# Six attention phases in a slot pipeline: one score round with 64 rows and 512 columns, v by one full-array product, layer normalisation on ScalarE

## The reference

```
def _mha(q, k, v, mask, ...):
    Q, K, V = (t @ w + b).reshape(b, s, H, DK).transpose(0, 2, 1, 3)   # for each of the three
    scores = einsum('bhqd,bhkd->bhqk', Q, K) / sqrt(DK)
    scores = where(mask[:, None] == 0, -1e20, scores)
    A = softmax(scores, axis=-1)
    return einsum('bhqk,bhkd->bhqd', A, V).transpose(0, 2, 1, 3).reshape(b, sq, D) @ wo + bo

def _ln(x, g, b):
    m, v = mean(x, -1), var(x, -1)
    return (x - m) * rsqrt(v + 1e-5) * g + b
```

## Time and profile before

| | |
|---|---|
| median of 3 runs | 714.12 us (712.08 to 714.96) |
| the profiled execution | 715.84 us, of which its span is 714.0 us |
| PE busy | 660.5 us (92% of the span) |
| DVE / ACT / POOL busy | 510.5 / 455.2 / 320.0 us |
| chain that ended last | PE 71%, issue 14%, POOL 7% |

### The profile page before, as it was taken

The page is one execution under the profiler, slowest core; times in us unless marked ns, Lnnn a source line. Parts: engine busy times, 40 slices in busy tenths (PEclk is TensorE's granted clock), DMA queues, the critical chain, the costliest instruction groups (busy, mean ns, idle before and its releaser), DMA issues.

```text
span 714.0 us, 26835 instructions
## 1 busy us (share of the span) xinstructions
PE 660.5 (92%) x9470; PEld 468.4 (66%) x9470; DVE 510.5 (71%) x1259; ACT 455.2 (64%) x1274; POOL 320.0 (45%) x540
## 2 busy tenths in 40 slices
PE   1999999999999999999999849899997899999995
PEld 1566666677777766666666536799993556666773
DVE  0599899878788778888888743344433788988884
ACT  1366777677777787777777533455524667777874
POOL 2244444467666653333377564255433345442110
PEclk9999999999999999999999769999995899999998
DMA  8333343322332310101011000122232000000100
GB/s 268 104 93 88 85 94 79 73 64 50 78 96 84 104 54 25 29 24 32 24 43 37 25 31 31 50 67 64 68 90 81 24 25 23 22 17 17 36 28 27
DMA packets 48527, 42.07 MB, mean 59 GB/s; under 512 B 6553, under 2 KB 42909, under 8 KB 47280
## 3 DMA queue, kind: packets, MB, share of 16 engines
q1 hardware_dynamic: 41632, 23.33, 11.6%
q10 hardware_dynamic: 4528, 13.25, 7.5%
q0 software_dynamic: 2272, 4.24, 1.9%
HBM read 25.41 MB, written 14.79 MB: 56 GB/s over the span
## 4 chain that ended last, share of the span: by engine, by line
PE 71%; issue 14%; POOL 7%; DVE 3%; ACT 2%; ACTq 1%; DMA 0%; SPq 0%; POOLq 0%; DVEq 0%
PE ps L570 11%; PE ps L607 10%; PE ps L738 5%; PE ps L811 5%; PE ps L800 5%; PE ps L663 5%; PE ps L644 4%; PE ps L680 4%; PE ps L746 4%; PE ps L719 3%; POOL k_by_j L500 3%; PE ps L664 2%; PE ps L766 2%; PE ps L592 2%; PE ps L691 2%
## 5 line engine op out<-in xcount | busy, mean ns | idle before, releaser
L1106 DVE TENSOR_REDUCE top<-ps 128x16 f32<-128x1024 f32 (+1 forms) x96 | 108.9, 1134 | 41.9 <-PE ps L570 40.2
L492 POOL TENSOR_TENSOR rstd<-spread,half_neg 128x1 f32<-128x1 f32 x80 | 44.5, 557 | 194.4 <-DVE spread L1199 115.2
L500 POOL TENSOR_TENSOR k_by_j<-k_t,cst 128x512 f32<-128x512 f32 (+1 forms) x96 | 95.5, 995 | 74.2 <-ACT k_t L915 37.8
L570 PE MATMUL ps<-k_by_j,q_t 32*64 32x256 f32 (+1 forms) x1536 | 125.2, 396 | 1.1
L607 PE MATMUL ps<-cst,prob 128*128 128x128 f32 x704 | 120.3, 291 | 1.1 <-ACT prob L936 1.0
L607 PEld LDWEIGHTS ps<-cst,prob 128*128 128x128 f32 x704 | 77.2, 144 | 62.0 <-issue 45.6
L1065 DVE RECIPROCAL inv<-ps 128x128 f32<-128x128 f32 x96 | 91.8, 956 | 32.3 <-PE ps L746 30.0
L1122 DVE TENSOR_TENSOR prob<-ps,top 128x1024 f32<-128x1024 f32 (+1 forms) x96 | 108.3, 1128 | 0.7
L936 ACT ACTIVATE prob<-prob 128x1024 f32<-128x1024 f32 (+1 forms) x96 | 94.8, 987 | 22.0 <-DVE prob L1122 21.7
L885 ACT ACTIVATE prob_t<-ps 128x512 f32<-128x512 f32 (+1 forms) x96 | 53.9, 561 | 38.7 <-PE ps L607 38.3
L873 ACT ACTIVATE prob_t<-ps 128x512 f32<-128x512 f32 (+1 forms) x96 | 53.9, 561 | 29.6 <-PE ps L607 28.5
(11 more groups left out here) (155 smaller groups left out, 1202.4 us busy)
## 6 DMA issues: line engine op xcount, KB each, us to landing
sorted_rows<-zero_rows ACTq DMA_DIRECT2D x32, 276.2 KB, 2.7
stage_m<-in_m SPq DMA_DIRECT2D x80, 64.0 KB, 1.9
mow<-in_mow SPq DMA_DIRECT2D x18, 256.0 KB, 3.0
stage_kv<-in_ctx_t SPq DMA_DIRECT2D x64, 64.0 KB, 1.7
rows_in<-sorted_rows SPq DMA_DIRECT2D x39, 65.0 KB, 1.8
wat<-in_wat ACTq DMA_DIRECT2D x1, 1280.0 KB, 6.5
x_t<-in_x_t SPq DMA_DIRECT2D x16, 64.0 KB, 1.9
stage_kv<-in_x_t SPq DMA_DIRECT2D x16, 64.0 KB, 1.7
```

What stands on the lines that cost most here:

```text
L500: pool.tensor_tensor(k_by_j[:, p, 0:nj, :], k_t[:, p:p + 1, :].broadcast_to([128, nj, TOK]), cst[:, cj:cj + nj].unsqueeze(2).broadcast_to( ...
L570: mm = pe.matmul(ps[S * b:S * b + S, 2 * p + bank, r * nj * S:(r + 1) * nj * S].rearrange("p (h k) -> p h k", k=S), q_t[rows_g, p, S * b:S ...
L1106: dve.tensor_reduce(top[:, p, 0:nh].rearrange("p (b h) -> p b h", b=2), sc, AX.X, ALU.max).then_inc(top_d, 1)
```

## The change

Three edits. **Scores:** `k_by_j` gets 8 copies for 16 heads (4 for 8 heads) in place of 4 (2). The scores are one round of four products with 64 rows and 512 columns (256 in phase 5) in place of two rounds of four with 32 rows and 256 (128) columns, and it stands whole at the head of the slot. Its waits are moved into the slot before, between the two groups of the last product (`score_ready(following)`). **v:** one product of the full array with 128 columns in place of four with 64 output columns; the copies to `v_16` and `v_8` then go from partition half b to half par, four in each phase (before: four with 16 heads, two with 8). **Normalisation:** in phases 0, 1 and 4 `normed` moves from DVE to ACT, as rstd*y + shift, where shift = -mean*rstd is made by two more small operations on POOL.

```
@@ gpsimd @@
                     pool.tensor_tensor(rstd[:, p, :], spread[:, p, :], half_neg[:, :], ALU.pow)\
                         .then_inc(rstd_d, 1)
+                    if POST[pr.phase] == "ln":
+                        pool.tensor_tensor(minus[:, p, :], none[:, :], moments[:, p, 0:1], ALU.subtract).then_inc(minus_d, 1)
+                    ...
+                        wait_pair(pool, minus_d, pr)
+                        wait_pair(pool, rstd_d, pr)
+                        pool.tensor_tensor(shift_n[:, p, :], minus[:, p, :], rstd[:, p, :], ALU.mult).then_inc(shift_d, 1)
                 pr = at(OFF_PROJ)
                 if pr is not None:
-                    p, nj = pr.p, heads(pr) // 4
+                    p, nj = pr.p, heads(pr) // 2
...
                     pool.tensor_tensor(k_by_j[:, p, 0:nj, :], k_t[:, p:p + 1, :].broadcast_to([128, nj, TOK]),
@@ tensor @@
+            def score(pr):
+                p, nj = pr.p, heads(pr) // 2
                 masked = MASKED[pr.phase]
                 for bank in range(2):
-                    rows_g = slice(32 * (2 * bank + r), 32 * (2 * bank + r) + 32)
+                    rows_h = slice(S * bank, S * bank + S)
                     for b in range(2):
                         mm = pe.matmul(
-                            ps[S * b:S * b + S, 2 * p + bank, r * nj * S:(r + 1) * nj * S].rearrange("p (h k) -> p h k", k=S),
-                            q_t[rows_g, p, S * b:S * b + S], k_by_j[rows_g, p, 0:nj, S * b:S * b + S],
-                            start=not masked and r == 0, stop=True, skip_group_check=True)
+                            ps[S * b:S * b + S, 2 * p + bank, 0:nj * S].rearrange("p (h k) -> p h k", k=S),
+                            q_t[rows_h, p, S * b:S * b + S], k_by_j[rows_h, p, 0:nj, S * b:S * b + S],
+                            start=not masked, stop=True, skip_group_check=True)
+                mm.then_inc(score_d, 1)
...
-                        scored = at(OFF_SCORE)
-                        if half == 0 and scored is not None:
-                            score_round(scored, 1).then_inc(score_d, 1)
...
-                    for b in range(2):
-                        for par in range(2):
-                            mm = pe.matmul(ps[S * par:S * par + S, B_PROJ, 256 + 64 * b:320 + 64 * b]
-                            ...
+                    mm = pe.matmul(ps[:, B_PROJ, 256:384], stage_kv[:, p, :], wat[:, ph, 2, :], start=True, stop=True)
...
+                    following = at(OFF_V)
+                    if following is not None:
+                        score_ready(following)
                     for k in range(step):
@@ scalar, behind the evacuation of the first half @@
+                pr = at(OFF_XT)
+                if pr is not None and POST[pr.phase] == "ln":
+                    wait_pair(act, xt_d, pr, 2)
+                    wait_pair(act, shift_d, pr)
+                    wait_pair(act, res_d, pr, 2)
+                    act.activation(normed[:, p, :], y[:, p, :], ACT.Identity, bias=shift_n[:, p, :], scale=rstd[:, p, :])\
+                        .then_inc(norm_d, 1)
@@ vector, behind heads_t @@
-                    dve.tensor_scalar(normed[:, p, :], y[:, p, :], moments[:, p, 0:1], rstd[:, p, :],
-                                      ALU.subtract, ALU.mult).then_inc(norm_d, 1)
```

More of the change, by code:

```diff
@@ L69 @@
 BIASED = {0: 0, 1: 1, 4: 2}
-C_ID, C_J16, C_J8, C_IOTA, C_BASE = 0, 128, 132, 134, 142
-C_STEP, C_UPTO, C_BLOCK = 150, 166, 230
+C_ID, C_J16, C_J8, C_IOTA, C_BASE = 0, 128, 136, 140, 148
+C_STEP, C_UPTO, C_BLOCK = 156, 172, 236
 C_O16 = C_BLOCK + JB
@@ L168, in build @@
         q_t, k_t = sb("q_t", [128, 2, TOK]), sb("k_t", [128, 2, TOK])
-        k_by_j = sb("k_by_j", [128, 2, 4, TOK])
+        k_by_j = sb("k_by_j", [128, 2, 8, TOK])
         prob = sb("prob", [128, 2, 16 * S])
@@ L493, in slot @@
                         .then_inc(rstd_d, 1)
+                    if POST[pr.phase] == "ln":
+                        pool.tensor_tensor(minus[:, p, :], none[:, :], moments[:, p, 0:1], ALU.subtract).then_inc(minus_d, 1)
+                    else:
+                        pool.sem_inc(minus_d, 1)
+                    if POST[pr.phase] == "ln":
+                        wait_pair(pool, minus_d, pr)
+                        wait_pair(pool, rstd_d, pr)
+                        pool.tensor_tensor(shift_n[:, p, :], minus[:, p, :], rstd[:, p, :], ALU.mult).then_inc(shift_d, 1)
+                    else:
+                        pool.sem_inc(shift_d, 1)
                 pr = at(OFF_PROJ)
                 if pr is not None:
-                    p, nj = pr.p, heads(pr) // 4
-                    cj = C_J16 if nj == 4 else C_J8
+                    p, nj = pr.p, heads(pr) // 2
+                    cj = C_J16 if nj == 8 else C_J8
                     wait_pair(pool, k_e, pr)
@@ L579, in slot @@
                 if pr is not None:
[L580 to L586, removed]
+                    if isinstance(pr.n, int):
+                        score_ready(pr)
+                    score(pr)
                 pr = follows(at, OFF_FY, FF)
@@ L665, in slot @@
                         .then_inc(proj_d, 1)
-                pr = at(OFF_SCORE)
-                if pr is not None and at(OFF_PV) is None:
-                    score_round(pr, 1).then_inc(score_d, 1)
                 pr = at(OFF_OUT)
@@ L942, in slot @@
                     wait_pair(act, pv_d, pr, 2)
-                    for par in range(2):
-                        rows_p = slice(S * par, S * par + S)
-                        src = ps[rows_p, B_PROJ, 256:384]
-                        if dk == 8:
-                            dst = v_16[rows_p, p, :, :, :].rearrange("r b (g k) c -> r (b g) (k c)", k=2)
-                            dst = dst.rearrange("r bg (k c) -> r bg k c", k=2)
-                            for k in range(2):
-                                ins = act.activation(
-                                    dst[:, :, k, 16 * k + 8 * par:16 * k + 8 * par + 8],
-                                    src.rearrange("r (bg k d) -> r bg k d", k=2, d=8)[:, :, k, :], ACT.Copy)
-                        else:
-                            ins = act.activation(
-                                v_8[rows_p, p, :, :, 16 * par:16 * par + 16].rearrange("r b q c -> r (b q) c"),
-                                src.rearrange("r (bq d) -> r bq d", d=16), ACT.Copy)
+                    for b in range(2):
+                        src = ps[S * b:S * b + S, B_PROJ, 256:384].rearrange("r (q par d) -> r q par d", par=2, d=dk)
+                        for par in range(2):
+                            rows_p = slice(S * par, S * par + S)
+                            if dk == 8:
+                                dst = v_16[rows_p, p, b, :, :].rearrange("r (g k) c -> r g (k c)", k=2)
+                                dst = dst.rearrange("r g (u w) -> r g u w", u=4)[:, :, 0:4:3, 8 * par:8 * par + 8]
+                                ins = act.activation(dst, src[:, :, par, :].rearrange("r (g k) d -> r g k d", k=2), ACT.Copy)
+                            else:
+                                ins = act.activation(v_8[rows_p, p, b, :, 16 * par:16 * par + 16], src[:, :, par, :], ACT.Copy)
                     ins.then_inc(v_e, 1)
@@ L1069, in slot @@
                         .then_inc(heads_d, 1)
-                pr = at(OFF_XT)
-                if pr is not None and POST[pr.phase] == "ln":
-                    p = pr.p
-                    wait_pair(dve, xt_d, pr, 2)
-                    wait_pair(dve, rstd_d, pr)
-                    wait_pair(dve, res_d, pr, 2)
-                    dve.tensor_scalar(normed[:, p, :], y[:, p, :], moments[:, p, 0:1], rstd[:, p, :],
-                                      ALU.subtract, ALU.mult).then_inc(norm_d, 1)
                 pr = follows(at, OFF_FN, FF)
```

32 lines of the change are left out of this document (16 added, 16 removed).

## The result

The changed kernel takes 721.94 us (median of 4 runs, 720.12 to 723.8), the kernel before 714.54 beside it: ratio 1.0113, 95% interval 1.0077 to 1.0149. It is slower, by 7.4 us where 19.3 had been forecast; 721.94 lies inside the stated range of 713 to 746, but the change is well under half of the one forecast. The profiled executions are 718.2 and 714.0 us of span, 4.2 apart, so the profiled one is among the quicker ones of the changed kernel.

What follows compares the result with a forecast made beforehand. It took TensorE's work, the transposes-ACT-output-product path and a feed-forward POOL-DVE loop as level bounds; 8.6 + 14.3 + 2.5 - 2.2 - 0.5 - 2.4 - 1.0 = +19.3 us gave 733 us, range 713 to 746.

Steps and rivals of the forecast that it cites:

- the loop: Feed-forward slots: `rstd`, `k_by_j`, `rstd_f`, `n_f`, `y` and the next `rstd` wait in turn, 7.43 us without room.
- Filling the pipeline: -1.0: At the kernel's start, filling the pipeline was to take 1.0 us less.
- I take -0.5: Router slots: gain from an earlier `score_d` and POOL's extra work cancel within -3 and +2 us; -0.5 taken.
- up to 0.4 a slot: Router slots: TensorE waits for DVE's ranks, which follow the scores; an earlier `score_d` gives up to 0.4 us a slot.
- rival 3: Feed-forward slots: idle TensorE's clock falls to 1.2 GHz; over 760 us if half of 16 slots; chance 0.03.
- 13 x 1.1 = +14.3: Feed-forward slots 24 to 36: longer `k_by_j` and two small POOL operations lengthen each by 1.1 us, +14.3 in all.
- The path over the transposes: Feed-forward slots: from `rrms_f`, two ACT operations and 1.4 us to the output product, less than 4 us from `n_f` to `y`.
- 32 x 0.27 = +8.6: Slots 5 to 23 and second group's 8 to 20: TensorE waits for `normed` on ACT, 5.58 against 5.31 us, +8.6.
- 14 x -0.17 = -2.4: Phase 5: TensorE saves 0.3 us a slot, ACT gets two more v copies, half comes through; -2.4 us.
- DVE gets lighter and gives nothing: Slots with layer normalisation: taking `normed` off DVE saves no time, as its `heads_t` is far ahead.
- Rival 2: All slots: TensorE's own work decides, 0.4 us less in 80 slots and 0.3 in 16, -37 us, 677; chance 0.14.
- At most 0.28: The v step: one full-array product takes at most 0.28 us against 0.38 for four products, 0.10 saved.

Runs made afterwards that it cites:

- early_norm: The changed kernel with `normed` on ACT moved ahead of the first evacuation of the transposes; 708.88 us, ratio 0.9934 to the kernel before.
- early_late: The changed kernel with `normed` ahead of the first evacuation and `k_by_j` of phases 1 and 2 one slot later; 699.13 us, ratio 0.979 to the kernel before.
- kj_late: The changed kernel with only `k_by_j` of phases 1 and 2 issued one slot later, behind the small normalisation operations; 717.38 us, ratio 1.0038 to the kernel before.
- no_v: The changed kernel with `normed` ahead of the first evacuation, `k_by_j` of phases 1 and 2 one slot later, v edit undone; 697.57 us, ratio 0.9731.
- b_alt: The kernel before with its four copies of v reordered so that the partition half changes with each copy; 716.44 us, ratio 1.0028.

## Why the prediction was wrong in size

**Right.** The scores group at 1.02 (forecast 1.03), the transposes' start to the first evacuation 0.75, `normed` at T+1.24, 0.48 long, TensorE waiting in front of it; slots of 5.52 to 5.63 (5.58); rms slots of 4.95 to 5.01 (5.03); `k_by_j` at 1.90 (1.90); the loop in the feed-forward slots and POOL without a gap in it. That TensorE's 92% were not the bound was right; early_norm and early_late show it by taking one wait each. Adding the two moves made the kernel 2.1% faster than before (interval 1.8 to 2.4%), without a single product less than in the changed kernel.

**The terms of the sum that were mis-sized.** The forecast sum was +19.3, the profiles differ by 4.2.

1. *"Filling the pipeline: -1.0", "I take -0.5" for the router, and nothing for the experts' part.* Measured -4.9 up to slot 5, -4.1 and -6.3, 14 us more gain than forecast and most of the miss. Their price was worked out at one clock, and the experts' part was put at nothing. The trace of before has half clock in them, and the changed kernel spends less time in it. By slot and by kernel that accounts for 2.6 of the router's 4.1 and for most of the experts' 6.3; at the start it fits but isn't separated from the shorter filling. No run changed the clock alone. Most of the router's rest is at full clock: 1.9 gained in slots 54 to 58, which is the "up to 0.4 a slot" of the prediction, and 0.6 lost in 59 to 63, whose cause no run shows. The prediction looked at the clock only for a fall in the feed-forward slots (rival 3).
2. *"13 x 1.1 = +14.3".* The loop shown grew by 0.78 (8.21 for 7.43), slots 26 to 36 by 0.84 in the mean. Against the forecast 1.1 there are 0.42 for the two small operations where I took 0.50, 0.59 from `rstd_f` to `n_f` where I kept 0.72, and 0.37 given back between `n_f` and `y` (3.67 for 4.04), where I allowed 0.27 at most and took 0.24. Slot 24, counted in full, grew by 0.22. One slot, the first with `xn_f`, took 10.83 instead of 7.39; TensorE idles 2.4 us there and its next group (line 692) goes at half pace, 1.92 us for eight where later ones take 1.08. This is rival 3 in one slot (the clock column has 0.50 from 157 to 160), and it brought the stretch to +12.7 after all: right in sum by luck. The path over the transposes was also nearer than I put it: I took it for clearly the shorter one, and kj_late, without the loop, still takes 8.07.
3. *"32 x 0.27 = +8.6".* I set 5.58 against the 5.31 of one slot. In the kernel before, slots lie between 5.30 and 5.46, 5.34 in the mean; measured +0.22 in the first group. Slots 6 to 24 and the second group's 4 to 20 together give +6.3 where 9.5 had been put.
4. *"14 x -0.17 = -2.4" in phase 5.* Measured +1.0 in slots 21 to 34. Four copies take 0.91 us on ACT where two took 0.54, 0.36 more, and the slots grow by as much. The scores' saving does come through by itself (3.70 us a slot with the scores alone, 3.99 before), and the copies take it back (4.05 with all three; no_v, without the v edit, has 3.70). I had the number of copies, but let half of TensorE's saving through without pricing them.

**A remark that was wrong.** I noted that "DVE gets lighter and gives nothing". Its relief was needed: beside the longer `k_by_j`, `normed` on VectorE makes the slot 5.97 us long, and 5.57 on ACT, 0.4 less. The forecast for the whole change, where `normed` is on ACT, didn't rest on it. The one for the scores alone did: 5.97 us where some 5.2 was expected, and so +11 us instead of 0 to +6.

**Numbers of the prediction that don't come out.** The bounds given add up to 720 to 748, not 746. Rival 2 needs the first evacuation at about T, not at T+0.4: 0.50 to `normed` and 0.485 of its own leave nothing of 1.0, so it deserved less than 0.14. "At most 0.28" for a full-array product isn't what half of 0.71 gives; the v product of the changed kernel takes mostly 0.22 to 0.30 up to the next group. None of these is a term of the sum.

**The second rival.** By the rule on drains in the Trainium skill, page TensorEngine Tiling (Array Packing), section Tiling Modes, the kernel would have become faster. The runs show that the wait behind the group decides: v alone removes a change of the tiling mode in each slot, and its slots with layer normalisation stay at 5.30 to 5.45.

## What to carry to other kernels

A matrix engine that is busy 99% of the time can still have a path of equal length beside it. Before work is taken from it, count from the start of a transposes group through each in-order queue to the wait that ends last; work that looks like load may be the cover of an evacuation. Where an operation on GpSimd gets longer, look at who stands behind it in its own queue, and at VectorE operations from SBUF to SBUF that run at the same time: here `normed` waited for its end. Two level paths have to be cut together; one alone shows little.

## What the runs showed of the hardware

- A VectorE `tensor_scalar` from SBUF to SBUF (0.34 us alone) that starts with 0.3 us or more of a GpSimd `tensor_tensor` ahead of it ends 0.08 to 0.09 us behind that instruction: 1.29 us beside one of 1.90, 0.97 or 0.43 beside two of 1.02.
- ACT copies of 64 x 64 elements from PSUM, 0.22 us each, follow each other at 0.12 us within a half of the partitions and at 0.22 to 0.23 when the half changes from one to the next; a change of the half that is written is enough.
- The scores in four quarters of the array take 1.02 us with 64 rows and 512 columns, against two rounds of 0.59 with 32 rows and 256 columns.
- The stretches at 1.2 GHz came back within 1 us of place and length in a second profile of the kernel before, but moved in the router's and the experts' part with as little as the order of four copies (b_alt). At the start of the second group there are 20.5 us in a row at half clock in the five profiles with two score rounds, 3.4 to 6.8 in the eight with one.
